# Softmax division moved ahead of the transposes in a pipelined scan and attention kernel (Trainium2, one core)

## What is computed

```python
# L2: q, k, v are 1x1 projections of xf (128 x 1024)
energy = einsum('bci,bcj->bij', q, k)
attention = softmax(energy, axis=-1)
out = einsum('bcj,bij->bci', v, attention)
out = gamma[0] * out + xf
# L3
scores = einsum('nia,nib->nab', theta, phi) / sqrt(c)
attn = softmax(scores, axis=-1)
f = einsum('nab,nib->nia', attn, g)     # then conv_w, batch norm, + x
```

## Time and profile before

| | |
|---|---|
| median of 3 runs | 5767.16 us (5764.43 to 5773.00) |
| profiled execution | 5769.15 us, its span 5767.4 us |
| VectorE busy | 5074.8 us (88%) |
| POOL busy | 4708.2 us (82%) |
| TensorE busy | 4678.8 us (81%) |
| ScalarE busy | 3719.5 us (64%) |
| granted TensorE clock, mean | 0.946 of full speed |

### The profile page before, as it was taken

The page is one execution under the profiler, slowest core; times in us unless marked ns, Lnnn a source line. Parts: engine busy times, 40 slices in busy tenths (PEclk is TensorE's granted clock), DMA queues, the critical chain, the costliest instruction groups (busy, mean ns, idle before and its releaser), DMA issues.

```text
span 5767.4 us, 61917 instructions
## 1 busy us (share of the span) xinstructions
PE 4678.8 (81%) x17331; PEld 2709.8 (47%) x17331; DVE 5074.8 (88%) x5978; ACT 3719.5 (64%) x6077; POOL 4708.2 (82%) x3342
## 2 busy tenths in 40 slices
PE   6568888888888888888888888888888888888771
PEld 6134454445445444544454454445444544544451
DVE  4699999999999999999999999999999999999933
ACT  3466666667666766666666667666666766666633
POOL 0698888898888889888988888888889888888810
PEclk9689999999999999999999999999999999999995
DMA  4465555555655555555655555655555555555527
GB/s 129 181 225 220 216 202 217 220 219 207 220 220 216 207 218 219 211 211 220 223 205 214 221 218 208 220 219 201 215 219 219 207 220 220 219 203 220 213 82 295
DMA packets 199100, 1216.87 MB, mean 211 GB/s; under 512 B 27881, under 2 KB 28657, under 8 KB 67697
## 3 DMA queue, kind: packets, MB, share of 16 engines
q1 hardware_dynamic: 194416, 1196.26, 56.1%
q10 hardware_dynamic: 4352, 16.78, 0.7%
HBM read 1158.43 MB, written 54.53 MB: 210 GB/s over the span
## 4 chain that ended last, share of the span: by engine, by line
PE 42%; DVE 25%; issue 15%; ACT 10%; POOL 6%; DMA 1%; DVEq 0%; SPq 0%; POOLq 0%; ACTq 0%
PE psA L814 14%; PE psE L814 13%; DVE psD L484 9%; DVE hs L488 8%; PE psT L814 6%; PE psT L987 4%; DVE nm L513 4%; ACT p L726 4%; POOL pa L300 3%; PE psY L814 3%; ACT da L680 2%; ACT L649 1%; ACT pt L690 1%; DVE psU L477 1%; POOL pa L306 1%
## 5 line engine op out<-in xcount | busy, mean ns | idle before, releaser
L300 POOL TENSOR_TENSOR pa<-hs,rows_all 128x1024 f32<-128x1024 f32 x1024 | 2411.4, 2355 | 530.6 <-DVE hs L488 529.6
L680 ACT ACTIVATE da<-delta,neg_a 128x512 f32<-128x512 f32 x2048 | 1380.2, 717 | 290.4 <-DVE hs L488 278.3
L484 DVE TENSOR_TENSOR psD<-rows_all,psU 128x512 f32<-128x512 f32 x2048 | 1415.1, 691 | 84.5 <-POOL hlast L304 6.2
L488 DVE TENSOR_TENSOR_SCAN hs<-da,hlast,psD 128x512 f32<-128x512 f32 x1024 | 1310.9, 1280 | 36.3
L306 POOL TENSOR_TENSOR pa<-pa 128x512 f32<-128x512 f32 x1024 | 1299.5, 1269 | 40.1
L488 DVE TENSOR_TENSOR_SCAN hs<-da,psD 128x512 f32<-128x512 f32 x1024 | 1249.5, 1220 | 35.2
L814 PE MATMUL psA<-pt,va 128*128 128x256 f32 x4096 | 947.4, 379 | 1.0 <-DVE x L531 0.6
L726 ACT ACTIVATE p<-psE,nm 128x1024 f32<-128x1024 f32 x512 | 571.2, 1116 | 493.4 <-DVE nm L513 493.4
L814 PEld LDWEIGHTS psA<-pt,va 128*128 128x128 f32 x4096 | 763.2, 190 | 178.8 <-issue 91.5
L513 DVE TENSOR_REDUCE nm<-psE 128x1 f32<-128x1024 f32 x512 | 618.7, 1208 | 216.5 <-PE psE L814 216.1
L690 ACT ACTIVATE pt<-psT 128x512 f32<-128x512 f32 x1024 | 559.0, 596 | 373.1 <-PE psT L987 361.6
(11 more groups left out here) (186 smaller groups left out, 5121.6 us busy)
## 6 DMA issues: line engine op xcount, KB each, us to landing
rows_all<-bc_scratch SPq DMA_DIRECT2D x1024, 1024.0 KB, 4.7
xin<-x SPq DMA_DIRECT2D x40, 512.0 KB, 7.7
xres<-x SPq DMA_DIRECT2D x64, 256.0 KB, 6.2
x_scratch<-x SPq DMA_DIRECT2D x32, 512.0 KB, 4.3
f_scratch<-fa SPq DMA_DIRECT2D x32, 512.0 KB, 6.8
xres<-x SPq DMA_DIRECT2D x8, 512.0 KB, 3.7
x1g<-x SPq DMA_DIRECT2D x8, 512.0 KB, 3.6
fa<-x SPq DMA_DIRECT2D x8, 512.0 KB, 3.6
```

The costliest lines, as they stand in the source:

```text
L300: pool.tensor_tensor(pa[:, k % PROD, :, :], hs[:, sl, :, :], rows_all[:, slot, 2:4, :], ALU.mult).then_inc(S["prod"], 1)
L484: dve.tensor_tensor(psD[:, :], rows_all[:, slot, j, :], psU[:, :], ALU.mult).then_inc(S["dbu_ok"], 1)
L488: dve.tensor_tensor_scan(hs[:, sl, j, :], da[:, sl, j, :], psD[:, :], hlast[:, h, n_:n_ + 1] if ch else 0.0, ALU.mult, ALU.add).then_inc(S ...
L680: act.activation(da[:, k % 2, j, :], delta[:, h, cols(ch)], ACT.Exp, scale=neg_a[:, h, 2 * q + j:2 * q + j + 1]).then_inc(S["da_ok"], 1)
```

## The change

The division moves from the end of the attention to the front of the transposes. VectorE takes a reciprocal for every tile (RECIP_AT now has eight entries, 16 reciprocals of one column for an image where there were 8 of two). It stands between the second multiplication and the second scan of a step; `scans` is split into `inputs` and `states` for that. ScalarE's new `scale` multiplies the tile p (128x1024) in place by the reciprocal, ahead of `turned_out`, and `turn` waits for it. The spreading matmuls, rb and its copy go, and VectorE's three operations on psA too. In their place gamma goes into the copy of va (m = 0), TensorE adds x1g by one matmul with the identity (m = 0), and ScalarE copies psA to x2 or fa (`weighed`). Three matmul groups change places in ORDER.

```diff
-        rb = sb("rb", [128, GL])
...
-            rb_ok=NG, q_mm=1, k_mm=2, v_mm=2, q_ok=1, k_ok=2, v_ok=2,
-            e_mm=16, nm_ok=16, p_ok=16, turn=32, pt_ok=32, rinv_ok=NG, av_mm=NG,
-            scaled=NG // 2, out_ok=NG, bn_ok=NG // 2,
+            q_mm=1, k_mm=2, v_mm=2, q_ok=1, k_ok=2, v_ok=2,
+            e_mm=16, nm_ok=16, p_ok=16, turn=32, pt_ok=32, rinv_ok=16, scaled=16, av_mm=NG,
+            out_ok=NG, bn_ok=NG // 2,
         )
...
         TURN_AT = [8, 10, 12, 12, 14, 15, 17, 18]
-        RECIP_AT = [10, 12, 15, 18]
+        RECIP_AT = [8, 9, 11, 12, 14, 15, 17, 18]
         WEIGH_AT = [(11, 12), (14, 15), (17, 18), (19, 19)]
...
+        def tiles_at(table, o):
+            return [(m, t) for m in range(2) for t in range(TILES) if 16 * m + table[t] == o]
         def turned_at(o):
-            return [(m, t) for m in range(2) for t in range(TILES) if 16 * m + TURN_AT[t] == o]
+            return tiles_at(TURN_AT, o)
         def groups_at(table, o):
...
-                def scans(b, k, j):
+                def inputs(b, k, j):
                     ch, r = divmod(k, NS)
...
                     dve.tensor_tensor(psD[:, :], rows_all[:, slot, j, :], psU[:, :], ALU.mult).then_inc(S["dbu_ok"], 1)
+                def states(b, k, j):
+                    ch, r = divmod(k, NS)
+                    h, q = divmod(r, PAIRS)
+                    sl = k % 2
                     wait(dve, "dbu_ok", b, 2 * k + j + 1)
...
                 def normalise(a, o):
-                    for m, gq in groups_at(RECIP_AT, o):
-                        i = NG // 2 * m + gq
-                        pair = slice(GT * (i % 2), GT * (i % 2) + GT)
-                        wait(dve, "p_ok", a, GT * (i + 1))
-                        wait(dve, "av_mm", a, i - 1)
-                        dve.reciprocal(rinv[:, pair], rsum[:, pair]).then_inc(S["rinv_ok"], 1)
+                    for m, t in tiles_at(RECIP_AT, o):
+                        i = TILES * m + t
+                        sl = slice(i % (2 * GT), i % (2 * GT) + 1)
+                        wait(dve, "p_ok", a, i + 1)
+                        wait(dve, "scaled", a, i - 2 * GT + 1)
+                        dve.reciprocal(rinv[:, sl], rsum[:, sl]).then_inc(S["rinv_ok"], 1)
                 def row_max(a, o):
...
                         part = slice(gq * GL, (gq + 1) * GL)
-                        wait(dve, "av_mm", a, i + 1)
-                        wait(dve, "rb_ok", a, i + 1)
-                        if m == 0:
-                            if gq == 0:
-                                at(dve, "x2_out", a * 16)
-                            wait(dve, "x1g_ok", a, NCH)
-                            dve.scalar_tensor_tensor(out=psA[:, 0:GL], in0=psA[:, 0:GL], scalar=c_gam, in1=rb[:, :],
-                                                     op0=ALU.mult, op1=ALU.mult).then_inc(S["scaled"], 1)
-                            wait(dve, "scaled", a, gq + 1)
-                            dve.tensor_tensor(x2[:, part], psA[:, 0:GL], x1g[:, part], ALU.add).then_inc(S["out_ok"], 1)
-                        else:
-                            if gq == 0:
-                                at(dve, "f_out", a * 16)
-                            dve.tensor_tensor(fa[:, part], psA[:, 0:GL], rb[:, :], ALU.mult
-                                              ).then_inc(S["out_ok"], 1)
+                        if m == 1:
                             wait(dve, "out_ok", a, i + 1)
...
                             if scan:
-                                scans(b, k, 0)
+                                inputs(b, k, 0)
+                                states(b, k, 0)
                             if front_of and r == AT_N:
                                 normed(*front_of)
-                            for a, o in now:
-                                normalise(a, o)
                             if att and k == 2:
...
                             if scan:
-                                scans(b, k, 1)
+                                inputs(b, k, 1)
+                            for a, o in now:
+                                normalise(a, o)
+                            if scan:
+                                states(b, k, 1)
                             for a, o in now:
...
                 def value(a, m):
...
                     wait(act, "v_mm", a, m + 1)
-                    act.activation(va[:, :, :], split(psT), ACT.Copy).then_inc(S["v_ok"], 1)
+                    if m == 0:
+                        act.activation(va[:, :, :], split(psT), ACT.Copy, scale=c_gam).then_inc(S["v_ok"], 1)
+                    else:
+                        act.activation(va[:, :, :], split(psT), ACT.Copy).then_inc(S["v_ok"], 1)
                 def residual(b, ch):
...
                         wait(act, "turn", a, 2 * (i - 1))
-                        wait(act, "rinv_ok", a, i // GT - 1)
+                        wait(act, "rinv_ok", a, i - 2 * GT + 1)
                         act.activation(p[:, i % 2, :], flat(psE), ACT.Exp, bias=nm[:, i % 2:i % 2 + 1],
...
-                def spread(a, o):
+                def scale(a, o):
+                    for m, t in tiles_at(RECIP_AT, o):
+                        i = TILES * m + t
+                        rs = i % (2 * GT)
+                        wait(act, "rinv_ok", a, i + 1)
+                        act.activation(p[:, i % 2, :], p[:, i % 2, :], ACT.Copy, scale=rinv[:, rs:rs + 1]
+                                       ).then_inc(S["scaled"], 1)
+                def weighed(a, o):
...
                         i = NG // 2 * m + gq
+                        part = slice(gq * GL, (gq + 1) * GL)
                         wait(act, "av_mm", a, i + 1)
-                        wait(act, "out_ok", a, i)
-                        act.activation(rb[:, :], psA[:, GL:2 * GL], ACT.Copy).then_inc(S["rb_ok"], 1)
+                        if gq == 0:
+                            at(act, ("x2_out", "f_out")[m], a * 16)
+                        if m == 1:
+                            wait(act, "bn_ok", a - 1, gq + 1)
+                        act.activation((x2, fa)[m][:, part], psA[:, 0:GL], ACT.Copy).then_inc(S["out_ok"], 1)
                 def image(b, scan, more, att, late):
...
                             for a, o in now:
-                                spread(a, o)
+                                weighed(a, o)
                             if att and k == 5:
...
                             for a, o in now:
+                                scale(a, o)
                                 turned_out(a, o)
...
                 def turn(a, m, t, front):
                     i = TILES * m + t
-                    wait(pe, "p_ok", a, i + 1)
+                    wait(pe, "scaled", a, i + 1)
...
                     for j in range(TB // 2 * half, TB // 2 * (half + 1)):
-                        last = mm(psA[:, 0:GL], va[:, j, :], pt[:, i % 2, j, :], start=(j == 0), stop=(j == TB - 1))
+                        last = mm(psA[:, 0:GL], va[:, j, :], pt[:, i % 2, j, :], start=(j == 0),
+                                  stop=(j == TB - 1 and m == 1))
                     if half:
-                        wait(pe, "rinv_ok", a, i + 1)
-                        for u in range(GT):
-                            rs = (GT * i + u) % (2 * GT)
-                            last = mm(psA[:, GL + 128 * u:GL + 128 * u + 128], rinv[:, rs:rs + 1].to_broadcast([128, 128]),
-                                      ident[:, :])
+                        if m == 0:
+                            wait(pe, "x1g_ok", a, NCH)
+                            last = mm(psA[:, 0:GL], ident[:, :], x1g[:, gq * GL:(gq + 1) * GL], start=False)
                         last.then_inc(S["av_mm"], 1)
...
                 def project(a, m, front, beside):
...
                     "energy turn add skip0",
-                    "gates add rows",
-                    "energy turn add",
-                    "energy steps add weigh0",
+                    "gates add",
+                    "energy rows turn add",
+                    "steps energy add weigh0",
                     "turn weigh1 turn_more skip1 add",
...
                     "energy turn weigh0 add",
```

## The result

The changed kernel took 6123.65 us in the median (6108.2 to 6129.7, 6 runs) against 5765.8 us of the kernel before in the same session (5764.14 to 5773.25). The ratio is 1.0612, 95% interval 1.0599 to 1.0625. It is 358 us slower. The direction was forecast, the size was not: 189 us were forecast, and 6124 lies above the range's end of 6050.

A forecast was written before the change was run, and what follows sets the result against it. VectorE was nearest to a bound, but TensorE's unbroken chain in steps 0 to 7 would set the pace: +2.1 and +3.4 us per half, +171 us over 31 images, +18 for the last, from 5769.15 to 5958 us; range 5660 to 6050.

The forecast's parts named there:

- VectorE's work: VectorE, per image: 5.3 us removed, 1.2 us of reciprocals added, net 4.1 us saved, a gain only where VectorE sets the pace.
- The scaling's duration: ScalarE's multiplication of a 128x1024 tile: 1.15 us each, bounds 1.00 and 1.15, about 1.05 in a stream of instructions.
- Late by 1.9 us at tile 5: Dense steps: ScalarE's full queue delays the scaling, so `turn` of tile 5 starts at 2083.15 instead of 2081.29.
- TensorE's clock: Matmuls behind TensorE's idle gaps may run near half clock, 3.34 against 1.73 us; counted as nothing in the sum.
- Rival B: TensorE: the new gaps also bring its clock down, 149 us on top, about 6105 us; chance 0.08.
- The tail: End of a pass: TensorE idle 1.8 us ahead of tile 6 and 1.5 us ahead of tile 7, waiting for scalings.
- How many links a shorter scaling shortens: Scalings of 1.00 us would take 0.15 us from each of two to three links per half, 25 us in all.
- The 0.9 us of `project`: TensorE's `project` no longer waits for VectorE, taking 0.9 us off the half in which m = 0 ends.
- The order: Three moved matmul groups: 2.07 us wait at tile 2 removed, 1.4 us added at tile 3; both halves gain about 2 us.
- The last image: The image without scans: each tile's chain gets a reciprocal and a scaling, 0.15 + 1.15 us, +18 us for 14 tiles.
- The signs: Profile after: VectorE under 90% busy, longer energy waits (2 to 3 us at tile 6), ScalarE 79%, steady image about 172 us.
- Rival A: Whole kernel: VectorE stays the bound and keeps its savings, 5580 us, or 5675 with half of them; chance 0.33.

The follow-up runs named there:

- e1: The kernel before with only the new order of the three matmul groups; 5754.5 us, ratio 0.9982.
- e12: The kernel after without the scaling and its hand-over, so nothing is divided by the row sums; 5659.5 us, ratio 0.981.
- e3: The kernel after with the scaling cut to 16 of a tile's 1024 columns, all hand-overs kept; 5878.1 us, ratio 1.0193.
- e8: The kernel after with five unused matmuls ahead of the softplus projections and five in the wait for scaled tile 5; 5981.0 us, ratio 1.0371.
- e11: The kernel before, in its own order, with five unused matmuls ahead of the rows projection; 5682.4 us, ratio 0.9847.
- e4: The kernel before with the same 16 ScalarE multiplications per image added, into a buffer nobody reads or waits for; 5968.4 us, ratio 1.0352.
- e9: The kernel before with the new order of the three matmul groups and five unused matmuls ahead of the softplus projections; 5656.0 us, ratio 0.9806.

## Why the prediction went as it did

Four steps lead from before to after:

| from | to | us | what it is |
|---|---|---|---|
| before 5766 | e1 5754.5 | -11 | order of the matmul groups |
| e1 | e12 5659.5 | -95 | VectorE's operations gone, TensorE's residual, ScalarE's copies |
| e12 | e3 5878 | +219 | hand-over of every tile, and a scaling of 0.30 us |
| e3 | after 6124 | +246 | length of the scaling, 0.30 to 1.145 us |

- **What bounds it, and where:** right. The time went into steps 0 to 7 and into VectorE's wait for energies, and the scalings of tiles 5, 6 and 7 are in the chain.
- **VectorE's work:** the size is right (5850 instructions, 128 fewer). I said its savings would vanish inside TensorE's chain. They do with the scaling in place; without it three quarters of them reach the time.
- **The scaling's duration:** 1.145 us measured, 1.15 taken. Gamma in va's copy added 0.09 us, 0.38 was right for the copies of psA.
- **Late by 1.9 us at tile 5:** the schedule by hand is for the half in which pass m = 0 begins, and it put `turn` of tile 5 at 2083.15, 42.3 us after the copy of du into psU that begins step 8 (2040.83). In the means of 24 steady images it came 40.6 us after that copy before, 43.7 after the change and 43.0 in e8. In the other half it was 39.8, 44.4 and 42.5. So my schedule was 1.4 us early in its own half. The clock explains about half of that; the rest stays open.
- **TensorE's clock:** this is the step that failed. "I have counted nothing for it in the sum; it is a rival below." In the kernel after it costs 143 us, the difference to e8. In steady half images this reads: 2.1 and 3.4 us longer were forecast, 5.1 and 6.5 were measured, and 3.6 and 3.3 in e8. So the waits of the sum were about right, and what was added up at nothing is most of the miss.
- **Why it was put at nothing:** I took the fall for something that the wait ahead of energy 7 brings, and judged that a shorter wait there would bring less. My own rows had both cases. Behind 2.08 us of idle energy 7 took 3.34 us in one half and 1.98 in the other. I also looked ahead of tiles 6 and 7, where 1.5 us of idle left the clock alone. It fell behind the waits for tile 1's copy and for scaled tile 5, 2.40 and 2.36 us. The first of these is in my text ("which in turn wait for tile 1's copy"), but only its length was added up.
- **Rival B** had 0.08. It had the kind of cause, and its 149 us on top lies close to the 143. That closeness is luck: 149 was three falls of 1.6 us at tiles 6 and 7, where the clock held.
- **What the 143 us are not:** they are not what the change added in slow clock. The kernel before loses to the clock too, 86 us by e11. With fillers in both kernels the change costs 299 us (5682.4 to 5981.0), more than the 189 of my sum. The sum started from a time with falls in it (5769.15) and followed a schedule without any.
- **The tail:** tiles 6 and 7, 1.8 and 1.5 us, were 1.51 each.
- **How many links a shorter scaling shortens:** I had two to three per half. The 246 us from e3 to the kernel after, divided by 0.84 us and 62 halves, make 4.7, and the chain above has six. What falls of the clock add to the 246 us was not separated.
- **The 0.9 us of `project`:** wrong. I let it go with VectorE's L531, which the profile named. It stays at 0.88 us after the change (at 2055.27), where L531 no longer exists. In the code this projection also waits until ScalarE has copied xc out of psT, and that copy started at 2054.48 for 0.69 us. Of two waits that ended together I took the named one away. 31 x 0.9 = 28 us. e8 lies 5981.0 - 5765.8 = 215 us above the kernel before, against my 189. The 28 us would fill that difference, which was not tried by itself.
- **The order:** right in sign for e1 (a small gain), and blind to what it does with the scalings in place (115 us).
- **The last image:** from the last scan to the end 263.6 us before, 274.1 after, so 10.5 us where I had 18.
- **The signs:** VectorE's busy share fell to 84%, its waits for energy 0 grew to 2.40 and 2.88 us, and it waits for energies 3 and 6, as forecast. The 2 to 3 us at tile 6 were 4.51 and 3.96. ScalarE came to 73% of the steady part and not 79%, since a steady image took about 178 us and not 172.
- **Rival A** had 0.33. The faster half of the change exists (e12, which divides nothing), but the division takes it back four times over.

What stays open: how the 219 us of the hand-over divide between clock falls and the plain wait. The granted clock of the steady part was 0.95 in e12 and in e3, so there was hardly more slow clock in all. Whether it moved to where others wait was not tried; e3 and e12 were not run with fillers. e4 says that load alone, with no hand-over, costs 203 us; the terms of the table are differences along one path, and along another they would be cut otherwise.

## What to carry to other kernels

An operation put between two engines that already hand tiles to each other can cost its length and a hand-over for most tiles, even where the engine that does it is idle a third of the time. Follow the last tiles of a pass through the queues, because what stands behind them has little slack (at most 1.7 us here). When a hand schedule opens a new wait of TensorE, price the matmuls behind it at both clock levels before giving that case a small chance. Do the same with the kernel that you start from, or the two will be compared at different clocks. Where a wait has two sources in the code and the profile names one, keep the other in the sum.

## What was not expected of the hardware

Adding matmuls that nobody uses made three kernels faster. Five of them (2.37 us) in one wait per half took 99 us from e1 (5754.5 to 5656.0) and 86 from the kernel before (5768.0 to 5682.4); five in each of two waits per half took 143 from the kernel after. The granted clock of the steady part rose from 0.96 to 0.99 in the last case. Behind idle times of 1.40 to 1.51 us transposes kept 1.09 us; behind 2.36 us they took 1.44 and 1.97. The same idle length does not always end the same way: behind 2.40 us the softplus projections took 3.08 us in one half and 1.95 in the other, with energy 3 at 3.78 and 3.26. In e9 energy 3 took 3.60 us right behind fillers and projections at full clock, with no idle time of its own. Nor does the mean clock order the kernels by time: e12 with 0.95 was 108 us faster than the kernel before with 0.97.
